# Attention masks applied as a 0/1 multiplication after the exponential instead of as added matmuls before it

## What is computed

```python
WINDOW = 512; HEADS = 8; DIM_HEAD = 64
q, k = l2norm(q) * qs, l2norm(k) * ksc       # per head of 64
q, k = rotary_xpos(q, k)
# for windows of 512 queries, keys of the own and the previous window:
sim = jnp.einsum('bhwid,bhwjd->bhwij', bq, bk)
mask = (i < j) | (i > j + WINDOW) | (j == -1)
sim = jnp.where(mask, -jnp.finfo(sim.dtype).max, sim)
attn = jax.nn.softmax(sim, axis=-1)
out = jnp.einsum('bhwij,bhwjd->bhwid', attn, bv)
```

## Time and profile before

| | us |
|---|---|
| median of 2 runs | 3905.07 (3904.08 to 3906.07) |
| time of the profiled execution | 3912.23 |
| its span on core 3, the slowest | 3910.5 |
| spans of the eight cores | 3876.4 to 3910.5 |
| PE busy in the span | 2781.9 (71%) |
| DVE busy | 1467.9 (38%) |
| ACT busy | 562.1 (14%) |
| mean granted TensorE clock of the cores | 0.732 to 0.739 |

### The profile page before, as it was taken

The page is one execution under the profiler, slowest core; times in us unless marked ns, Lnnn a source line. Parts: engine busy times, 40 slices in busy tenths (PEclk is TensorE's granted clock), DMA queues, the critical chain, the costliest instruction groups (busy, mean ns, idle before and its releaser), DMA issues.

```text
span 3910.5 us, 35380 instructions; the slowest of 8 cores (3876.4 to 3910.5 us)
## 1 busy us (share of the span) xinstructions
PE 2781.9 (71%) x10940; PEld 1049.5 (27%) x10940; DVE 1467.9 (38%) x2161; ACT 562.1 (14%) x860; POOL 516.6 (13%) x933
## 2 busy tenths in 40 slices
PE   2667984657878874389999656778777536999970
PEld 1312331222222222034334322222222202343420
DVE  2685663662223224322321366332232323232116
ACT  0011121111211120211001011112211121011101
POOL 3000001000000001243333100000000033335210
PEclk9987996765555558599999777555555758999975
DMA  7100002000000000665565200000000064667522
GB/s 107 26 1 8 14 17 49 1 1 0 1 1 1 1 1 14 98 95 87 71 93 72 43 1 1 1 1 1 0 1 1 11 101 68 81 82 111 70 50 86
DMA packets 136867, 143.15 MB, mean 37 GB/s; under 512 B 33436, under 2 KB 115356, under 8 KB 136688
## 3 DMA queue, kind: packets, MB, share of 16 engines
q0 software_dynamic: 129632, 128.01, 22.5%
q1 hardware_dynamic: 7056, 12.88, 1.0%
HBM read 249.90 MB, written 12.58 MB: 67 GB/s over the span
## 4 chain that ended last, share of the span: by engine, by line
PE 57%; DVE 21%; issue 7%; DMA 7%; ACT 5%; POOL 3%; DVEq 1%; ACTq 0%; SPq 0%; POOLq 0%
PE pA L1036 6%; PE pG L1041 6%; PE pP L277 5%; PE pX3a L1092 4%; PE pX3b L1092 4%; PE pAV L712 3%; DVE g2f L298 3%; DMA W1g<-w_i 3%; PE pST L729 2%; PE pST L732 2%; PE pS L729 2%; PE pS L732 2%; PE pWo L809 2%; PE pS L646 1%; PE pST L646 1%
## 5 line engine op out<-in xcount | busy, mean ns | idle before, releaser
L1036 PE MATMUL pA<-HN,W1a 128*128 128x512 bf16 (+1 forms) x1408 | 348.2, 392 | 74.7 <-DMA W1g<-w_i 43.8
L1041 PE MATMUL pG<-HN,W1g 128*128 128x512 bf16 (+1 forms) x1408 | 340.4, 386 | 0.0
L1060 DVE SCALAR_TENSOR_TENSOR HG<-pA,b1ac,scr 128x512 bf16<-128x512 f32 (+1 forms) x176 | 132.1, 750 | 548.9 <-ACT scr L1055 548.9
L1018 POOL DMA_DIRECT2D W1a<-w_i x384 | 238.2, 620 | 679.3 <-PE pG L1041 677.2
L774 DVE CAST Arbc<-pS 64x512 bf16<-64x512 f32 x32 | 21.8, 682 | 696.5 <-PE pS L769 696.5
L1022 POOL DMA_DIRECT2D W1g<-w_i x384 | 241.4, 629 | 29.8 <-issue 29.7
L1055 ACT ACTIVATE scr<-pG,b1gc 128x512 bf16<-128x512 f32 (+1 forms) x176 | 120.9, 687 | 823.7 <-PE pG L1041 823.7
L508 PE MATMUL pQKV<-AQ,XT 128*128 128x512 bf16 x768 | 230.9, 473 | 8.8 <-DVE rope L482 8.8
L792 POOL DMA_DIRECT2D AO<-wo_i x8 | 4.3, 561 | 1699.7 <-DVE AoT L777 1699.7
L1036 PEld LDWEIGHTS pA<-HN,W1a 128*128 128x128 bf16 (+1 forms) x1408 | 138.7, 100 | 257.1 <-issue 113.6
L277 PE MATMUL pP<-WqkvT,XT 128*128 128x512 bf16 x768 | 191.0, 394 | 0.0
(11 more groups left out here) (240 smaller groups left out, 3567.7 us busy)
## 6 DMA issues: line engine op xcount, KB each, us to landing
W1a<-w_i POOLq DMA_DIRECT2D x320, 128.0 KB, 6.1
W1g<-w_i POOLq DMA_DIRECT2D x320, 128.0 KB, 6.4
W2i<-w_i POOLq DMA_DIRECT2D x42, 256.0 KB, 16.4
wst<-Wqkv POOLq DMA_DIRECT2D x24, 256.0 KB, 3.7
AQ<-wqkv_i POOLq DMA_DIRECT2D x16, 384.0 KB, 14.7
XS<-x POOLq DMA_DIRECT2D x16, 256.0 KB, 15.3
x1h<-XS SPq DMA_DIRECT2D x16, 256.0 KB, 2.0
out<-of_sb SPq DMA_DIRECT2D x8, 512.0 KB, 3.2
```

The lines of the kernel that those rows point to most:

```text
L1018: E("ge", lambda e, j=j, b5=b5, wa=wa, l=l, bb=bb: e.dma_start(out=W1a[bb][:, 512 * j:512 * j + wa], in_=self.dw1[l, 128 * j:128 * (j + 1) ...
L1036: ins = e.matmul(pA[pp][0:wh, :], W1a[bb][:, 512 * j + 128 * i5:512 * j + 128 * i5 + wh], HNc[:, 512 * j:512 * (j + 1)], start=(j == 0), s ...
L1041: ins = e.matmul(pG[pp][0:wh, :], W1g[bb][:, 512 * j + 128 * i5:512 * j + 128 * i5 + wh], HNc[:, 512 * j:512 * (j + 1)], start=(j == 0), s ...
```

## The change

The triangles are no longer added to the scores. In the maximum part, L649, L654 and L660 go: the maximum is taken over all scores of the tiles, the masked ones too. In the output part, L734 and L743 go, so the exponential is also taken of masked scores. A new SBUF tile `m01` holds the exponentials of `cmTA` and `cmTB`, that is 0 and 1; two Scalar engine instructions make it once in `phase_WA`, as soon as the constants are loaded. After each exponential the Vector engine multiplies the first 128 columns of `APT` by the one triangle, in place, and, where the tile has 640 columns, the last 128 by the other. `av` waits for the last of these products instead of for the exponential.

```diff
--- before.py
+++ after.py
@@ -138,6 +138,7 @@
         self.cones16 = self.sb(s, "k_cones16", [128, 128], FP16)
         self.zros = self.sb(s, "zros", [128, 512])
         self.scr = [self.sb(s, f"scr{i}", [128, 1024]) for i in range(4)]
+        self.m01 = self.sb(s, "m01", [128, 256])
         self.stat = self.sb(s, "stat", [128, 24], F32)
         self.of_sb = self.sb(s, "of_sb", [128, 1024], F32)
 
@@ -209,6 +210,9 @@
                          (self.cI16, self.dI16), (self.cones16, self.dones16)):
             E("sy", lambda e, d=dst, s=src: e.dma_start(out=d[:], in_=s), inc=[("dy", 16)])
         dy_consts = C["dy"]
+        E("se", lambda e: e.activation(self.m01[:, 0:128], self.cmTA[:], AF.Exp),
+          wait=[("dy", dy_consts)])
+        E("se", lambda e: e.activation(self.m01[:, 128:256], self.cmTB[:], AF.Exp))
 
         for t in range(NT):
             E("ge", lambda e, t=t: e.dma_start(
@@ -625,6 +629,7 @@
         pAV = self.ps(stP2, "pAV" + L, [65, 2048])
 
         se_exp = {}
+        ve_mask = {}
         ve_oT = {}
         pe_av_last = {}
         for h in range(HEADS):
@@ -645,20 +650,14 @@
                     if t >= 4:
                         e.matmul(pbuf[:, 0:512], qsl,
                                  AkT[base:base + 64, 2048 * g + kstart:2048 * g + kstart + 512],
-                                 start=True, stop=False)
-                        e.matmul(pbuf[:, 0:128], self.cI[:], self.cMA[:],
-                                 start=False, stop=True)
-                        e.matmul(pbuf[:, 512:640], qsl,
-                                 AkT[base:base + 64, 2048 * g + kstart + 512:2048 * g + kstart + 640],
-                                 start=True, stop=False)
-                        ins = e.matmul(pbuf[:, 512:640], self.cI[:], self.cMB[:],
-                                       start=False, stop=True)
+                                 start=True, stop=True)
+                        ins = e.matmul(pbuf[:, 512:640], qsl,
+                                       AkT[base:base + 64, 2048 * g + kstart + 512:2048 * g + kstart + 640],
+                                       start=True, stop=True)
                     else:
-                        e.matmul(pbuf[:, 0:wdt], qsl,
-                                 AkT[base:base + 64, 2048 * g:2048 * g + wdt],
-                                 start=True, stop=False)
-                        ins = e.matmul(pbuf[:, wdt - 128:wdt], self.cI[:], self.cMB[:],
-                                       start=False, stop=True)
+                        ins = e.matmul(pbuf[:, 0:wdt], qsl,
+                                       AkT[base:base + 64, 2048 * g:2048 * g + wdt],
+                                       start=True, stop=True)
                     return ins
                 E("pe", p1, wait=w, inc=[("pe", 1)])
                 pe_p1 = C["pe"]
@@ -715,7 +714,7 @@
                                        stop=stop)
                         pos += take
                     return ins
-                E("pe", av, wait=[("se", se_exp[(h, kc)])], inc=[("pe", 1)])
+                E("pe", av, wait=[("ve", ve_mask[(h, kc)])], inc=[("pe", 1)])
                 pe_av_last[(h, kc)] = C["pe"]
 
             for kc in range(NT):
@@ -729,18 +728,15 @@
                     e.matmul(stb[:, 0:wA], ksl,
                              AqT[base:base + 64, 2048 * g + 128 * kc:2048 * g + 128 * kc + wA],
                              start=True, stop=False)
-                    e.matmul(stb[:, 0:wA], self.cones[0:1, :],
-                             Anegm[0:1, 128 * kc:128 * kc + wA], start=False, stop=False)
-                    ins = e.matmul(stb[:, 0:128], self.cI[:], self.cmTA[:],
+                    ins = e.matmul(stb[:, 0:wA], self.cones[0:1, :],
+                                   Anegm[0:1, 128 * kc:128 * kc + wA],
                                    start=False, stop=True)
                     if wq > 512:
                         e.matmul(stb[:, 512:640], ksl,
                                  AqT[base:base + 64, 2048 * g + 128 * kc + 512:2048 * g + 128 * kc + 640],
                                  start=True, stop=False)
-                        e.matmul(stb[:, 512:640], self.cones[0:1, :],
-                                 Anegm[0:1, 128 * kc + 512:128 * kc + 640],
-                                 start=False, stop=False)
-                        ins = e.matmul(stb[:, 512:640], self.cI[:], self.cmTB[:],
+                        ins = e.matmul(stb[:, 512:640], self.cones[0:1, :],
+                                       Anegm[0:1, 128 * kc + 512:128 * kc + 640],
                                        start=False, stop=True)
                     return ins
                 E("pe", p2, wait=w, inc=[("pe", 1)])
@@ -752,6 +748,15 @@
                     APT[kc % 2][:, 0:wq], stb[:, 0:wq], AF.Exp),
                   wait=w)
                 se_exp[(h, kc)] = C["se"]
+                E("ve", lambda e, kc=kc: e.tensor_tensor(
+                    APT[kc % 2][:, 0:128], APT[kc % 2][:, 0:128],
+                    self.m01[:, 0:128], op=OP.mult),
+                  wait=[("se", se_exp[(h, kc)])])
+                if wq > 512:
+                    E("ve", lambda e, kc=kc: e.tensor_tensor(
+                        APT[kc % 2][:, 512:640], APT[kc % 2][:, 512:640],
+                        self.m01[:, 128:256], op=OP.mult))
+                ve_mask[(h, kc)] = C["ve"]
                 if kc > 0:
                     emit_av(kc - 1, min(640, T - 128 * (kc - 1)))
             emit_av(NT - 1, min(640, T - 128 * (NT - 1)))
```

## The result

| | before | changed |
|---|---|---|
| median | 3912.06 us (10 runs) | 3851.23 us (12 runs) |
| lowest | 3902.41 | 3810.82 (one more execution, listed beside these, took 3807.71) |
| ratio, 95% interval | | 0.978 (0.974 to 0.983) |
| the same comparison repeated (first experiment; chip 0, the record doesn't name the first one's) | 3917.92 (11 runs) | 3810.72 (7 runs), 0.973 (0.968 to 0.978) |
| mean span of the eight cores in the profile | 3895.2 | 3808.1, and 3784.0 in the first experiment |

The change makes the kernel faster by 2.2% in the first measurement and 2.7% in the repeat. The first one's interval reaches from 0.974 to 0.983, so it can't tell whether the gain is above 2%; that of the repeat ends at 0.978. I had forecast 3.3% and 3778 us, with a range to 3812.

The account below looks back on a forecast made before the run. Matmuls at half clock, in loops with other engines, bound the heads; saving (3.3 + 4.6) x 16 = 126.4 us, less 1.4, taken as 127, gives 3905 - 127 = 3778 us. Range 3750 to 3812 (8 in 10), the forecast's own 3755 to 3800.

Parts of the forecast that it names:

- the products are hidden in the middle turns: Output part: exponential, products and hand-overs take 2.08 us against 2.13 us available, so the masks are hidden by 0.05 us.
- the last five turns of an output part: Output part, av of kc 10 to kc 15: from 6.55 to 6.7 us, 0.15 lost because av waits in nearly every turn.
- the first head of a layer: Output part: the 1.28 us table load is no longer covered by p2, some 0.7 us lost, twice per kernel.
- The path L: Output part, start of p2's last matmul to its av, through exponential and both products: 2.08 us, before 1.35.
- Nothing else changes: Normalising part, projections and feed-forward part: same instructions and waits, so no term in the sum.
- the slowest core can be another (the spans lie within 34 us): Whole kernel: a reason given for the forecast's own range of 3755 to 3800 us.
- Without L734 and L743 it is 0.43 to 0.44 shorter: Output part: the turn from av to av falls from 2.48 to 2.045 us, if the added work fits.
- my own sign for it: Output part: a turn of 2.05 to 2.09 us was to show the forecast right.
- The last matmul is then L651, which starts ... 0.53: Maximum part: 0.53 us after L646 instead of 0.95, so the two-tile loop falls from 2.88 to 2.46, taken as 2.44.
- the longer path: Output part, rival 1: exponential, products and hand-overs take 2.5 instead of 2.08 us, turn 2.23, kernel 3831 us; 9%.
- DVE would hold the maximum part where it was: Maximum part, rival 2: no gain there, 53 us missing, kernel 3831 us; 5%.
- The clock did not rise: Output part, rival 4: granted clock rises to 1.00, turn 1.50 us, 96 us more saved, about 3680 us; 3%.

Follow-up runs that it names:

- first experiment: The changed kernel unaltered, run again alternating with the kernel before on one chip: 3810.72 against 3917.92 us, ratio 0.973 (0.968 to 0.978).

## Why the prediction was off

Right: that all of it happens in the heads, that the clock there stays at 0.50, that the normalising part keeps its 12.88 us, and that the products are hidden in the middle turns. Right too were the small terms: the last five turns of an output part got 0.1 us longer (6.54 to 6.63, forecast 0.15), and the first head of a layer gains some 0.75 us less than the others (forecast 0.7). The product takes 0.225 us, as interpolated from the earlier trace rows:

```profile
L751 DVE TENSOR_TENSOR APT<-APT,m 128x128 bf16<-128x128 bf16 x256 | 57.7, 225 | 418.9 <-ACT APT L747 418.9
```

The path L was 2.02 instead of 2.08 us at the start of an output part, where nothing hides it, and the first `av` came 3.30 us after the first matmul instead of 3.36:

```profile
1023.71 0.60 PE L728 MATMUL pST<-AqT,AkT 64*128 64x512 f16 x1
1025.21 0.60 PE L728 MATMUL pS<-AqT,AkT 64*128 64x512 f16 x1
...
1027.01 0.71 PE L711 MATMUL pAV<-APT,Av 128*65 128x512 bf16 x2 [0.22 <-DVE APT L756]
```

Wrong, in order of size:

- **The time of the slowest core was taken as the time of an undisturbed one.** This is the step that took the forecast out of its range: "Nothing else changes" outside the heads, and "the slowest core can be another (the spans lie within 34 us)". The 3778 is close to what cores show (they average 3784 in the first experiment, 3808 in the profile), but the metric is the slowest of eight, and in the profile of the first measurement it was held back by feed-forward stretches at 0.81: core 5 took 608 us where cores 2 and 3 took 537 and 538. The sum had no term for it, and the range, 34 us upward, had only the spread of one execution, though the trace of before already had 88 to 104 us at 0.81 on six of its cores. Between 3778 and 3851 us lie: 15 from the mis-sized heads (112 saved instead of 127), 7 from the kernel before (3912 instead of 3905), and another 51. That these 51 come from such stretches is argued from the one profile (309 us at 0.81 instead of 1.00 are 58 us) and not shown for the median. In the repeat, where the changed kernel's profile shows none, the median was 3811: 33 above 3778, of which the heads are 15, the kernel before 13 (3918 instead of 3905) and 5 are left. Why such stretches come in one execution and not in the next is open. The Trainium skill (TensorE: Matmul & The Clock Gate, section "Seeing it yourself") describes a current limit per die, to 13/16 of the clock, when three of its cores or more run dense matmuls. The granted 0.81 agrees with 13/16. The rest isn't borne out here: all eight cores run the same dense part in every execution, cores 2 and 3 of this profile never dropped to 0.81 while cores 0 and 1 of the same die had 189 and 207 us of it, and cores 4 and 5 had three times as much as 6 and 7.
- **"Without L734 and L743 it is 0.43 to 0.44 shorter"**: it was 0.30. I took out the 0.215 between L740 and L743 and kept the 0.08 from L743 to `av`, as if any matmul ahead would hide that weight load; L738 doesn't, and the distance is 0.21. 0.135 us in ten turns and 16 heads are 22 us. The output part gained 3.27 us per head instead of 4.6, and the turn missed my own sign for it, 2.05 to 2.09. The line to look at was in the trace of before: the weight load of L712 started with L743's matmul, while those of L729, L732, L734, L737, L740 and L743 started behind the matmul ahead of them.
- **"The last matmul is then L651, which starts ... 0.53" after L646**: it was 0.39, for the same reason with the other sign, so the loop fell below DVE's own 1.19 and that became the bound. The maximum part gained 3.72 us instead of 3.3: 7 us back. That the two errors partly cancel is luck.

One slip is in the sum itself: 126.4 less 1.4 is 125, and I took 127, the upper end.

Of the rivals, the longer path did not come: L is short, and without any product the turn is the same. That DVE would hold the maximum part where it was did not come either, but it does hold it now, at 1.19 per tile. The clock did not rise: PE is busy 31.8 of 35 us in the output part, and the granted clock is 0.50.

## What to carry to other kernels

Before a matmul is taken out, look at the weight loads on both sides of it: a load that starts with the matmul ahead is hidden by it, and comes back on the path when that matmul goes. Where the tensor engine alternates between operands on different numbers of rows, grouping those on the same rows costs nothing and gave 2.3 us per head here; taking the triangle matmuls out of the same part gave 3.3. And where the time is that of the slowest of eight cores, a range needs the spread between executions, not only that between the cores of one; a granted clock below the usual one in a stretch of the trace of before is a sign of it.

## What the runs showed of the hardware

- A weight load starts with the matmul ahead of it if both are on the same rows (128 and 128: L743 to L712, L741 to L711; 64 and 64: L651 to L654, L728 to L732; one and one: L735 to L739), and the next matmul then comes after 0.38 to 0.40 us for 512 columns instead of 0.54. Where the rows change (64 to one, one to 64, one to 128), it starts behind. Each hidden load of 128 columns is worth 0.11 us net at a granted clock of 0.50. The Trainium skill (TensorE: Matmul & The Clock Gate, section "The mechanism") says that weight loads overlap running matmuls only where their row groups differ (its section "Step-by-step: what each phase is for" also allows it where the load goes to a background buffer). These rows go the other way on both sides: loads to the same rows are hidden, and in odd heads, where the scores lie on partitions 64 to 127 and the added maxima on partition 0, they are not, and the turn is the same 2.18 us as in even ones.
- At a granted clock of 0.50 an exposed weight load of 128 columns adds 0.11 us per matmul: a quarter of a 512-column matmul and as much as a 128-column one.
- A bf16 product of 128x128 in SBUF takes 0.225 us; one over two blocks of 128 columns saved 0.32 us per head against two of them.
- The granted clock has a value of 0.81 besides 0.50 and 1.00, for stretches of up to some 110 us (core 5 of the changed kernel from 1688 to 1800 us), on some cores and not on others of the same die and execution.
